# Keys by token and channels of x through 32x32 transposes and DMA, instead of transposes on TensorE

## What is computed

```python
x = L0_attn_x                                # (16, 1024, 512)
x = x + 0.5 * ffn(layernorm(x))              # first half
x = x + attn(layernorm(x))
x = x + 0.5 * ffn(layernorm(x))              # second half

def attn(x):                                 # 16 heads of 32 channels
    q, k, v = split(x @ w_attn)
    q, k = elu(q) + 1, elu(k) + 1
    # per head, causal over t: S += k_t v_t^T; z += k_t
    # y_t = (q_t S) / (q_t . z + 1e-6)
    return y @ w_proj

def ffn(x):                                  # 64 hidden channels, 16 relus on each
    s = x @ Win + bin_
    h = relu(s[..., None] * W1 + b1)
    g = sum(h * W2, -1) + b2
    return g @ Wout + bout
```

## Time and profile before

| | us |
|---|---|
| median of 3 executions | 2390.56 (2390.17 to 2390.65) |
| the profiled execution | 2391.91 |
| its span, first to last instruction | 2390.1 |
| PE busy | 2294.7 (96%) |
| DVE busy | 1940.2 (81%) |
| ACT busy | 1426.8 (60%) |
| POOL busy | 812.3 (34%) |

### The profile page before, as it was taken

The page is one execution under the profiler, slowest core; times in us unless marked ns, Lnnn a source line. Parts: engine busy times, 40 slices in busy tenths (PEclk is TensorE's granted clock), DMA queues, the critical chain, the costliest instruction groups (busy, mean ns, idle before and its releaser), DMA issues.

```text
span 2390.1 us, 74560 instructions
## 1 busy us (share of the span) xinstructions
PE 2294.7 (96%) x32450; PEld 1763.3 (74%) x32450; DVE 1940.2 (81%) x3346; ACT 1426.8 (60%) x2267; POOL 812.3 (34%) x864
## 2 busy tenths in 40 slices
PE   3999999999999999999999999999999999999995
PEld 3777777777777777777777777777777777777773
DVE  6678888888888888888888988888988888887766
ACT  5555656555656555656655656655656655656654
POOL 5233233333333333333333333333333333333311
PEclk7999999999999999999999999999999999999997
DMA  5001102111101111111111111111111111110110
GB/s 172 20 20 37 55 20 56 55 55 37 55 20 56 55 55 38 55 34 42 55 55 40 52 38 38 55 55 44 48 38 38 56 55 49 43 38 20 37 38 36
DMA packets 49592, 111.51 MB, mean 47 GB/s; under 512 B 8177, under 2 KB 10225, under 8 KB 45170
## 3 DMA queue, kind: packets, MB, share of 16 engines
q1 hardware_dynamic: 49266, 106.74, 15.3%
HBM read 72.12 MB, written 34.60 MB: 45 GB/s over the span
## 4 chain that ended last, share of the span: by engine, by line
PE 74%; DVE 15%; issue 4%; POOL 4%; ACT 1%; SPq 1%; DMA 0%; DVEq 0%; POOLq 0%; ACTq 0%
PE bank L993 33%; PE att L993 13%; PE att L1011 6%; PE att L1085 5%; PE att L1110 5%; DVE st L664 3%; DVE res L714 3%; DVE acc_psum L702 2%; PE att L1101 2%; PE bank L1036 2%; PE bank L1073 2%; POOL z L358 2%; PE att L1027 2%; PE bank L1121 1%; DVE xf L692 1%
## 5 line engine op out<-in xcount | busy, mean ns | idle before, releaser
L449 ACT ACTIVATE xhat<-res,nmr,rstd 128x512 f32<-128x512 f32 x384 | 302.2, 808 | 353.8 <-DVE nmr L672 291.0
L464 ACT ACTIVATE ffr<-ffs,b1c,w1c 128x512 f32<-128x512 f32 (+1 forms) x544 | 427.9, 812 | 20.5 <-DVE acc_psum L702 13.9
L702 DVE SCALAR_TENSOR_TENSOR acc_psum<-ffr,w2c,acc_psum 128x512 f32<-128x512 f32 (+1 forms) x510 | 382.6, 750 | 48.8 <-ACT ffr L464 27.6
L362 POOL TENSOR_SCALAR_AFFINE_SELECT A<-A 128x512 f32<-128x512 f32 x256 | 157.0, 638 | 705.0 <-ACT A L426 705.0
L350 POOL TENSOR_TENSOR res<-res,hbout 128x512 f32<-128x512 f32 x256 | 352.2, 1393 | 4.0 <-ACT xhat L449 3.4
L664 DVE BATCH_NORM_STATS2 st<-res 128x6 f32<-128x512 f32 x384 | 260.7, 679 | 16.7 <-DMA res<-in_L_attn_x_dram 11.0
L358 POOL TENSOR_TENSOR z<-qT,z 128x512 f32<-128x512 f32 x128 | 165.9, 1296 | 268.6 <-DVE zc L744 118.3
L993 PE MATMUL att<-xh,wa_h 128*128 128x512 f32 x584 | 235.2, 403 | 1.9 <-DVE xl L681 1.9
L993 PE MATMUL att<-xh,wa_l 128*128 128x512 f32 x584 | 231.3, 396 | 0.0
L993 PE MATMUL att<-xl,wa_h 128*128 128x512 f32 x584 | 231.2, 396 | 0.0
L993 PE MATMUL bank<-wa_h,xh 128*128 128x512 f32 x504 | 214.7, 426 | 0.5 <-issue 0.5
(11 more groups left out here) (128 smaller groups left out, 4967.2 us busy)
## 6 DMA issues: line engine op xcount, KB each, us to landing
res<-in_L_attn_x_dram SPq DMA_DIRECT2D x32, 1024.0 KB, 5.3
xf<-scratch SPq DMA_DIRECT2D x128, 256.0 KB, 4.4
out_dram<-res SPq DMA_DIRECT2D x32, 1024.0 KB, 4.7
scratch<-rden SPq DMA_DIRECT2D x128, 8.0 KB, 1.5
kT<-in_L_attn_w_attn_dram SPq DMA_DIRECT2D x1, 1024.0 KB, 5.3
qT<-in_L_attn_w_attn_dram SPq DMA_DIRECT2D x1, 1024.0 KB, 10.9
v<-in_L_attn_w_attn_dram SPq DMA_DIRECT2D x1, 1024.0 KB, 14.2
A<-in_L_attn_w_proj_dram SPq DMA_DIRECT2D x4, 256.0 KB, 14.0
```

The source lines that it names most:

```text
L362: eng.affine_select(out=A[:, h, :, :], in_=A[:, h, :, :], compare_op=ALU.is_ge, fill=0.0, base=0, pattern=[[0, 4], [1, P]], channel_multip ...
L449: eng.activation(xhat[t % 2][:, :], res[b % SLOTS][:, t, :], ACT.Identity, bias=nmr[:, n, b % 2, t:t + 1], scale=rstd[:, n, b % 2, t:t + 1 ...
L464: eng.activation(ffr[i % 2][p, :], ffs[p, :], ACT.Relu, bias=b1c[p, i:i + 1], scale=w1c[p, i:i + 1]).then_inc(s_hr, 1)
L702: eng.scalar_tensor_tensor(psum[p, :], r[p, :], w2c[p, i:i + 1], psum[p, :], ALU.mult, ALU.add).then_inc(s_hm, 1)
```

## The change

**Keys by token.** PE's four transposes of a key tile and ACT's copy are gone. DVE's `key(j, t)` transposes each 32x32 piece of `kT` into `ks`, which lies over `xf[0]` (free after `ff_in`). SP's `key_out` writes this to DRAM (one DMA of 256 KB), waits, and `key_in` reads it back in four DMAs of 64 KB in runs of 512 bytes, into one of now two `ktok` slots. `update` waits for that DMA.

**Channels of x.** For blocks 1 to 31 the four transposes per tile on PE are gone. DVE's `squares` transposes into the new `xs`; `chans_out` and `chans_in` bring it through DRAM into `xf[0]` in the same way, and ACT and DVE make `xh` and `xl` from there instead of from PSUM. The four DMAs of `chans_in` for one tile are like those of `key_in`.

**Key sums.** The scan writes four slots in `A`, the scores' buffer, instead of two in `z2`, so the scan waits for the last `attend` of the block before, and the copies and masks of the scores wait for `den`.

**Order.** `spread` is cut into `rec_out` and `rec_in`, and SP has an order of its own. All engines' lists are reordered. On PE the second product of a step's start is q's first group. `ff_in` comes between the projections and values, all four `den` stand together behind it, and `scores(j, 0)` follows at once.

```diff
+            def key_out(b, t):
+                n = nth_update(b, t)
+                e.wait_ge(s_kt, n)
+                e.wait_ge(s_ktok[n % 2], 64 * of_its_kind(n - 2))
+                eng.dma_start(keys[n % 2].rearrange("h i r n -> (h i) (r n)"), ks[:, t, :]).then_inc(s_kw[n % 2], 16)
+
+            def key_in(b, t):
+                n = nth_update(b, t)
+                s = n % 2
+                e.wait_ge(s_kw[s], 16 * of_its_kind(n))
+                e.wait_ge(s_up, n - 2)
...
+                for r in range(4):
+                    eng.dma_start(ktok[D * r:D * r + D, s, :].rearrange("i (h n) -> i h n", h=4),
+                                  keys[s, :, :, r, :].rearrange("h i n -> i h n")).then_inc(s_ktok[s], 16)
...
+            def squares(b, t):
+                n = 4 * (b - 1) + t + 1
+                e.wait_ge(s_xn[L2], 4 * b + t + 1)
+                e.wait_ge(s_xw[n % 2], 16 * of_its_kind(n - 2))
+                eng.transpose(xs[:, n % 2, :].rearrange("p (r k i) -> p k r i", r=4, k=KC),
+                              xhat[t % 2][:, :].rearrange("p (k r i) -> p k r i", r=4, k=KC)).then_inc(s_xT, 1)
...
+            def key(b, t):
+                w = slice(t * P, t * P + P)
+                e.wait_ge(s_elu[1], 4 * b + 4)
+                e.wait_ge(s_fi, b + 2)
+                e.wait_ge(s_xTl, 4 * b + t + 1)
+                eng.transpose(ks[:, t, :].rearrange("p (r g d) -> p g r d", r=4, g=4),
+                              kT[:, :, w].rearrange("p g (r i) -> p g r i", r=4)).then_inc(s_kt, 1)
...
             def update(b, t):
                 o = take("up", b, t)
-                e.wait_ge(s_ktok, nth_update(b, t))
+                s = nth_update(b, t) % 2
+                e.wait_ge(s_ktok[s], 64 * of_its_kind(nth_update(b, t)))
```

More of the change, by code:

```diff
@@ L870, in _ @@
                     hidden(j, 2)
+                if on(j) and updates(j, 3):
+                    key(j, 3)
+                if on(j - 1) or on(j + 2):
                     hidden(j, 3)
@@ L912, in _ @@
                 if on(j - 1) or on(j + 2):
-                    hidden(j, 13)
-                if on(j + 1):
-                    channels(j + 1, 1)
-                if on(j - 1) or on(j + 2):
-                    hidden(j, 14)
+                    hidden(j, 15)
+                if on(j):
+                    outer(j, 1)
+                if on(j) and updates(j, 3):
+                    update(j, 3)
                 if on(j):
@@ L1170, in _ @@
                 if on(j):
+                    den(j, 0)
+                    den(j, 1)
+                    den(j, 2)
+                    den(j, 3)
+                    scores(j, 0)
+                    values(j, 0, 1)
+                    values(j, 1, 0)
                     values(j, 1, 1)
-                    scores(j, 0)
+                    attend(j, 0)
+                    update(j, 0)
                     values(j, 2, 0)
                     values(j, 2, 1)
-                    attend(j, 0)
@@ L1176, in _ @@
-                    update(j, 0)
-                    key(j, 1)
+                    update(j, 1)
+                    scores(j, 1)
                     values(j, 3, 0)
+                    attend(j, 1)
                     values(j, 3, 1)
-                if on(j + 1):
-                    channels(j + 1, 0)
-                if on(j):
-                    scores(j, 1)
                     outer(j, 0, 0)
-                    attend(j, 1)
-                    update(j, 1)
+                    scores(j, 2)
@@ L1187, in _ @@
                     outer(j, 0, 1)
-                    key(j, 2)
-                    scores(j, 2)
-                    outer(j, 1, 0)
                     attend(j, 2)
                     update(j, 2)
+                if on(j) and updates(j, 3):
+                    update(j, 3)
+                if on(j):
+                    outer(j, 1, 0)
                     outer(j, 1, 1)
-                if on(j + 1):
-                    channels(j + 1, 1)
-                if on(j):
                     scores(j, 3)
@@ L1208, in _ @@
                 if on(j - 1) or on(j + 2):
-                    ff_out(j, 0)
-                if on(j) and updates(j, 3):
-                    key(j, 3)
-                if on(j):
-                    outer(j, 3, 1)
-                if on(j) and updates(j, 3):
-                    update(j, 3)
-                if on(j - 1) or on(j + 2):
-                    ff_out(j, 1)
                     ff_out(j, 2)
```

406 lines of the change are left out of this document (230 added, 176 removed).

## The result

The changed kernel takes 2747.8 us (median of 4 runs, 2744.1 to 2749.5) against 2390.6 for the kernel before: ratio 1.149, 95% interval 1.147 to 1.151. The forecast was 2635, its range ended at 2740. The sign and the place were right; the size was 113 us short.

A forecast was written before the change was run, and what follows sets the result against it. PE's issue, 72 us in each of 32 steps, was taken as the bound. Per step -4.2 +8.2 +2.1 +1.4 +0.2 = +7.7 us, +246 in all, gave 2635 us, range 2450 to 2740.

The forecast's parts named there:

- the fourth tile's keys: Keys arriving behind eight `chans_in` reads and a write needing `squares(3)`: 0.2 us wait per step, bounded by 0 and 1.
- What leaves PE: Key and channel transposes and gaps around the denominators removed from PE: 4.2 us less per step, 134 us in all.
- DVE's transposes at nothing: DVE's 7.5 more transposes per step, 4.5 us, costed at nothing on the path, covered by the waiting.
- The denominators' chain: Denominators, reciprocal, SP, DMA, `ynorm`, `yl`: `scores(1)` not before 45.0 us against PE's arrival at 40.0, a 5.0 us wait.
- The second tile's keys: `update(1)` waits 8.2 us per step for keys whose write stands behind the broadcast, landing at 47.8 us; 5.0 with overtaking.
- Rival 1: The second keys' write overtakes the broadcast, so only the denominators bind: 2535 us, or 2467 if the clock held; chance 0.28.
- The clock: A gap of 8 us in every step lowers PE's granted clock behind it: +2.1 us per step.
- `sums`, 1.4: `ff_out(0)` straight after `attend(3)` waits for `sums`, which stands behind `ynorm(3)` on DVE: 1.4 us per step.
- Start and end, nothing: Kernel's start and end change little, as their long waits are for data and for DVE.
- Rival 3: Each SP issue of a 64 KB read costs 0.6 us instead of 0.42: 2730 us and above; chance 0.09 beyond 2740.
- Rival 2: The round trip is hidden and the kernel is faster, 2300 us if the whole wait vanished; chance 0.15, 0.11 for faster.

The follow-up runs named there:

- e2: Changed kernel with `update` reading a constant array and `ynorm` multiplying by a constant, so neither waits for DMAs, which still run; 2378.0 us, ratio 0.994.
- v4: v2 with the eighth `ff_out` product given another bank and DVE's additions put ahead of the statistics; 2390.5 us, ratio 0.9996 to the kernel before.
- v5: v4 with half of `values(0)` ahead of the fourth denominators' product and the fourth tile's statistics one addition later; 2373.2 us, ratio 0.992.
- e1: Changed kernel with the state updates reading a constant array instead of `ktok`, so they wait for no keys; key DMAs still run; 2598.6 us, ratio 1.087.
- e5: Changed kernel with only SP's queue reordered: second keys' write and broadcast first, reads of first keys and channels behind; 2654.0 us, ratio 1.109.
- e7: Changed kernel with only `update(0)` reading a constant array and waiting for no keys; 2745.4 us, ratio 1.148.
- e6: Changed kernel with only `update(3)` reading a constant array and waiting for no keys, reads still issued; 2669.4 us, ratio 1.117.
- e3: Changed kernel with the second tile's keys written ahead of the denominators' broadcast read, nothing else; 2657.6 us, ratio 1.112.
- e4: Changed kernel with `sums` ahead of `ynorm(3)` in DVE's list; 2740.7 us, ratio 1.146.
- v2: Changed kernel with all engines' lists reordered, then denominators ahead of `values(0)`, `outer(3)` ahead of `ff_out`, and PSUM banks given out anew; 2569.1 us, ratio 1.074.

## Why the prediction fell short

By its own steps. Over the loop, the forecast had +7.7 us a step and the chip shows +11.0. The time lies just above the range, and what put it there is named below: above all the fourth tile's keys.

- **What leaves PE, -4.2.** Near: some 3.7 by e2. It is 16 us over the run.
- **DVE's transposes at nothing.** Right in the changed kernel, where DVE has time enough. In v4 and v5, with DVE at 86 and 87%, PE's largest wait is for DVE.
- **The denominators' chain, 5.0.** The chain was right, the size short: 6.9 (e1). In the step shown the broadcast starts 37.8 us into the step (forecast 37.2) and lands at 44.9 (42.9). The 5.7 from first issue to landing was itself wrong for the kernel before: I added the median of all four DMAs (4.4) to the issue of the last one. The last one takes 5.9 by its own median, and the four together 7.2, before (over 32 steps) as after. The eight reads ahead don't lengthen it; in e5, which has none there, it is 7.6. This misreading is 1.5 of the 1.9 us, and it runs on into the next term. (The lengths up to the end of `den` add up to 29.7, not 30.0; both chains are counted from there, so no wait changes.)
- **The second tile's keys, 8.2.** Right in mechanism, and near in size in part by luck: with 7.2 for the broadcast the same sum gives 9.7, and in e7, where as in the forecast nothing waits at `update(0)`, the wait is 9.2. In the changed kernel `update(0)` and `update(1)` together wait for 7.9 (252.3 over 32 steps in e6), and in the step shown `update(1)` starts 49.3 us into the step (`key_in(1)` was to land at 47.8). The choice between 5.0 and 8.2 is settled by e3: the write moved ahead of the broadcast gives back 90 us, 2.8 per step. The Trainium skill (DMA: Bandwidth & Descriptors, section "Queues, rings and completion order") has each DMA engine take the descriptors of one queue in ring order; the 5.8 us of this trace, against 2.2 in e3, agree with it. Rival 1, overtaking, is out.
- **`update(0)`, for which the sum had no term.** In my own layout PE reaches it at 36.4, and the last read of its keys is issued at 37.2; that alone told of a wait. The trace shows 2.5 on average, 3.5 in the step above. That I didn't look cost nothing: e7 shows that this wait is taken from that of `update(1)`.
- **The fourth tile's keys, 0.2. This step failed.** I bounded it by 0 and 1. It is 60 us of waits and 18 of clock, 78 us in all (e6), so 2.4 per step. In SP's rows above, the write of the fourth keys (L290 at 1446.01) is followed by eight reads for two tiles of `chans_in` that hold SP for 3.8 us, and the reads of the keys end at 1453.1; PE stood at `update(3)` from 1450.15. An estimate from these rows: with the 2.2 us of such a write the reads could have gone out at 1448.2, so the eight reads cost 2.1 us, and the four reads themselves held SP for 2.81 where those of the first tile held it for 1.86, 0.95 more. The rest of the 4.53 comes from further ahead: SP stood before `chans_out(3)` (L309 at 1441.78) until DVE had made `squares(3)`. I had named the eight reads and this write, and then judged by eye that PE comes about as late. But `update(3)` stands directly behind `update(2)`, and the scores of the fourth tile behind it. This one term is 72 of the 113 us that were missing; without it the time would be 2676, inside the range.
- **The clock, 2.1.** The mechanism was right, the count short, since there are two or three gaps in a step (2.5, 5.5 and 3.5 us on average) and not one of 8. The remainder of the step's 11.0 (less 9.7 for `ktok` and 1.5 for `sums`, and with 3.7 gained) is 3.5. In e7, with one gap fewer per step, the waits are 37 us longer (349.2 in total) and the time is the same, so the stretch behind `update(0)` is worth some 1.2 us on average, and in the changed kernel it costs no time, since the wait at `update(1)` is shorter by as much. The 3.5 is what is left over and wasn't measured by itself.
- **`sums`, 1.4.** Measured 1.5. That taking it away is worth that much is wrong: e4 gives back 7 us, not 45. The wait was priced rightly, what goes with it was not: the banks behind it come free no sooner.
- **Start and end, nothing.** 10.6 us: from the last but one copy of `ff_in`'s product to the end it is 90.1 in place of 76.2, and the start is 3.3 shorter.

Rival 3 (each issue costs more) came nearest in time and, but for one place, not in cause. Most reads of 64 KB held SP for 0.44 to 0.49 each, not 0.6; those of the fourth tile's keys, behind eight others, took 0.70 by their median. Rival 2, a hidden round trip, needs another order of PE: v4 and v5 are that kernel. So the loss of 357 us is not in the 32x32 transposes or in going through DRAM; it is in when PE asks for what comes back. What is open: v5 gains 19 us, where 118 (32 times 3.7) had left PE. PE's waits shown above for v5 add up to 101 us, about what is missing, most of them in the chain of scores, masks, `ynorm` and `yl` between PE and DVE, where taking one wait made another. Whether DVE's 125 us more keep them there no run shows, nor where their floor is. Nor was the kernel before tried with a new order of its own.

## What to carry to other kernels

Before work that covers a round trip is moved ahead of it, subtract: here 17.1 us of cover behind the denominators became 10.0 (by the forecast's layout), and `yl` was ready after 17.5 and the second keys after 19.9 (1416.5 to 1434.0 and to 1436.4). When a transfer is a set of DMAs, take the landing of the last one and not the median of the set: 5.9 and not 4.4 here. Price every consumer in the group, also the last, with all DMAs that stand ahead of it on its queue; waits whose landings hang on the same event replace each other (e7), the one whose landing doesn't adds up (e6). And a bank or a buffer given out in a ring is part of the order: one bank in the wrong place, and the statistics ahead of its emptying, cost 179 us between v2 and v4, more than all the transposes were worth.

## What the runs showed of the hardware

What I hadn't expected is how little idle time brings the lower clock. Busy time per stretch (length, then PE, PEld, DVE, ACT, POOL with instructions, granted clock, DMA share, GB/s), in the changed kernel the stretches right behind its gaps of 3.51 and 4.53 us:

```profile
1427.06:1431.90 4.84, 4.84 (x44) 3.66 (x44) 0.00 (x0) 0.00 (x0) 0.00 (x0) 0.65 0.96 243
...
1454.68:1459.00 4.32, 4.32 (x43) 3.56 (x44) 0.11 (x1) 0.00 (x0) 0.00 (x0) 0.64 0.00 0
```

Each is partly at the lower of the two levels (0.50, 1.2 GHz), and by 0.35 of 4.84 and 0.36 of 4.32 such a gap costs 1.6 to 1.7 us more than it lasts, where no later wait takes that up. Shorter gaps did it too, but not each. These are the stretches behind a wait of 1.89 us (at 361.12) and one of 1.87 us (at 605.98) in the same kernel, both at `update(0)`:

```profile
361.12:365.40 4.28, 4.28 (x42) 3.47 (x43) 0.00 (x0) 0.00 (x0) 0.00 (x0) 0.61 0.98 227
605.98:610.30 4.32, 3.46 (x44) 2.52 (x44) 0.00 (x0) 0.00 (x0) 0.00 (x0) 1.00 0.99 220
```

In e3 a wait of 3.12 us (before 1458.10) left the clock full. So the length of one gap doesn't settle it.

In v4, whose longest gap in mid-run is under 2 us, the mean granted clock is 0.985, that of the kernel before. Two new numbers are of DMAs. A write of 256 KB behind the broadcast took 5.8 us to landing in place of 2.2. And of four broadcast reads of 256 KB issued in a row, each took longer to its landing than the one ahead: 3.2, 4.1, 4.8 and 5.9 us by their medians over the 32 steps of the kernel before.
